# Two attentions in a hand-ordered kernel: row maxima 49 steps ahead of the scores instead of 64

## The reference

```
x = x + tanh(g_xattn[0]) * attention0(layernorm(x), context)     # 16 heads of 16, causal
x = x + tanh(g_ffn[0])   * moe0(layernorm(x))                    # 32 experts, top 8
x = x + tanh(g_xattn[1]) * attention1(layernorm(x), context)     # 16 heads of 16, row mask
x = x + tanh(g_ffn[1])   * moe1(layernorm(x))                    # 8 experts, top 2

scores  = q @ k.T / sqrt(16);  att = softmax(scores);  out = (att @ v) @ Wp + bp
```

## Time and profile before

| | us |
|---|---|
| median of three runs (2055.78 to 2060.46) | 2060.3 |
| the profiled execution, its own time | 2058.18 |
| its span, first to last instruction | 2056.1 |
| attention 0 with its set-up, about | 0 to 667 |
| experts 0, about | 667 to 902 |
| attention 1, about | 902 to 1574 |
| experts 1, about | 1574 to 2056 |
| mean granted TensorE clock | 0.946 |

### The profile page before, as it was taken

The page is one execution under the profiler, slowest core; times in us unless marked ns, Lnnn a source line. Parts: engine busy times, 40 slices in busy tenths (PEclk is TensorE's granted clock), DMA queues, the critical chain, the costliest instruction groups (busy, mean ns, idle before and its releaser), DMA issues. The chain is left out here.

```text
span 2056.1 us, 29834 instructions
## 1 busy us (share of the span) xinstructions
PE 1774.4 (86%) x10491; PEld 1061.7 (52%) x10491; DVE 1069.3 (52%) x2740; ACT 888.6 (43%) x1684; POOL 603.5 (29%) x580
## 2 busy tenths in 40 slices
PE   3799999889873999827899999999974999999995
PEld 1456555555542877713344444443332666666664
DVE  4556877787745644405877777778521122212221
ACT  3366665655541222223677777776750111111110
POOL 4222211210002678732211331231123244433322
PEclk9999999999985999968999999999986999999998
DMA  3535545334223788635323433332132133333314
GB/s 108 173 119 169 157 150 162 111 119 138 76 79 96 166 173 176 134 67 169 103 69 119 136 98 99 115 116 67 44 104 84 32 83 83 80 80 77 82 21 102
DMA packets 204243, 222.84 MB, mean 108 GB/s; under 512 B 33438, under 2 KB 195231, under 8 KB 203431
## 3 DMA queue, kind: packets, MB, share of 16 engines
q1 hardware_dynamic: 176458, 177.48, 28.3%
q0 software_dynamic: 27648, 43.60, 11.4%
HBM read 155.06 MB, written 86.93 MB: 118 GB/s over the span
## 5 line engine op out<-in xcount | busy, mean ns | idle before, releaser
L902 DVE TENSOR_REDUCE nmx<-mxb 128x1 f32<-128x512 f32 (+1 forms) x896 | 521.7, 609 | 238.9 <-PE mxb L673 145.8
L760 ACT ACTIVATE pt<-stb 128x512 f32<-128x512 f32 x832 | 475.2, 598 | 278.0 <-PE stb L693 154.4
L673 PE MATMUL mxb<-kst,qst 96*128 96x512 bf16 (+4 forms) x1024 | 334.6, 349 | 38.6 <-DVE nmx L902 28.2
L690 PE MATMUL stb<-qst,kst 99*128 99x512 bf16 (+4 forms) x1024 | 327.2, 344 | 8.6 <-DMA qst<-m3T 4.7
L706 PE MATMUL ob<-pt,va 128*32 128x512 f32 (+3 forms) x2048 | 220.1, 525 | 2.7 <-ACT pt L760 1.7
L690 PEld LDWEIGHTS stb<-qst,kst 102*128 102x128 bf16 (+1 forms) x1024 | 99.5, 99 | 213.5 <-ACT pt L760 136.7
L1192 POOL TENSOR_TENSOR qk<-qk,parts 128x512 f32<-128x512 f32 x64 | 73.0, 1161 | 431.0 <-ACT qk L795 226.2
L673 PEld LDWEIGHTS mxb<-kst,qst 99*128 99x128 bf16 (+1 forms) x1024 | 101.3, 99 | 152.1 <-DVE nmx L902 80.7
L1734 POOL DMA_INDIRECT x_after_l<-e_y,e_token x64 | 99.5, 1555 | 271.8 <-DVE e_y L1699 257.1
L1695 DVE TENSOR_TENSOR e_y<-e_y_bank,kst 128x512 f32<-128x512 f32 x32 | 22.1, 692 | 196.1 <-PE e_y_bank L1599 196.1
L1497 POOL DMA_INDIRECT x_after_l<-e_y,token x64 | 102.2, 1597 | 46.6 <-DMA x_after_l<-e_y,token 19.1
(11 more groups left out here) (252 smaller groups left out, 2959.2 us busy)
## 6 DMA issues: line engine op xcount, KB each, us to landing
qk_parts<-parts SPq DMA_DIRECT2D x16, 1536.0 KB, 6.3
qst<-qk_parts SPq DMA_DIRECT2D x384, 64.0 KB, 2.3
kst<-qk_parts SPq DMA_DIRECT2D x384, 64.0 KB, 2.3
rows<-rows SPq DMA_DIRECT2D x15, 1060.0 KB, 8.5
crow<-in_ctx SPq DMA_DIRECT2D x16, 512.0 KB, 3.9
x_after_l<-xres SPq DMA_DIRECT2D x16, 512.0 KB, 3.3
e_gu_nat<-in_L_ffn_gate_up_proj SPq DMA_DIRECT2D x64, 128.0 KB
qst<-in_L_ffn_w SPq DMA_DIRECT2D x8, 1024.0 KB, 7.2
```

Of the source, the lines that this page charges most:

```text
L673: last = pe.matmul(out, qst[par][0:rows_used, h, qt * P:(qt + 1) * P], kst[par][0:rows_used, h, 0:nk], start=True, stop=not causal)
L690: last = pe.matmul(bank[:, to:to + S - q_from(kt)], kst[par][0:ROWS, h, kt * P:(kt + 1) * P], qst[par][0:ROWS, h, q_from(kt):S], start=Tru ...
L760: act.activation(pt[:, slot(b, u), q0:S], stb[no % N_ST][:, q0:S], ACT.Exp, scale=SCALE).then_inc(s["st_free"], 1)
L902: last = dve.tensor_reduce(nmx[:, qt, h:h + 1], got[:, at:at + k_to(qt)], AX.X, ALU.max, negate=True)
```

## The change

The maxima run 15 steps later on every engine: `maxima(nxt, u - 15)` at step u, and the last 15 steps of an item are made in the item's own iteration, at steps 0 to 14. The steps of the shift move with them: first half - parts at 47 and 48, trip at 49, copy at 50; second half - parts at 15 and 16, trip at 17, copy at 18. Parts two and three now stand in one step, and the trip in the next. In SP's queue `load_ctx` goes ahead of `shift(cur, 1)`. Nothing is added or removed.

```diff
-    3: ("k", 2, 0, 0, 0), 4: ("k", 2, 0, 1, 0), 5: ("shift", 0, 1, 0, 1),
+    3: ("k", 2, 0, 0, 0), 4: ("k", 2, 0, 1, 0), 17: ("shift", 0, 1, 0, 1),
...
-    36: ("shift", 1, 0, 0, 0), 39: ("o", 0, 1, 0, 0), 40: ("y", -1, 0, 0, 1), 41: ("y", -1, 1, 0, 0),
+    49: ("shift", 1, 0, 0, 0), 39: ("o", 0, 1, 0, 0), 40: ("y", -1, 0, 0, 1), 41: ("y", -1, 1, 0, 0),
...
 STEPS = 64
+BEHIND = 15
...
                 if nxt is not None:
                     stack(nxt, 3)
+                if nn is not None and nn + 1 < B:
+                    load_ctx(nn + 1)
                 if cur is not None:
                     shift(cur, 1)
-                if nn is not None and nn + 1 < B:
-                    load_ctx(nn + 1)
...
                     if cur is not None:
                         scores(cur, u)
-                    if nxt is not None:
-                        maxima(nxt, u)
+                    if u < BEHIND and cur is not None:
+                        maxima(cur, u + STEPS - BEHIND)
+                    if u >= BEHIND and nxt is not None:
+                        maxima(nxt, u - BEHIND)
...
-                    if u == 6 and cur is not None:
+                    if u == 18 and cur is not None:
                         shift_out(cur, 1)
-                    if u == 37 and nxt is not None:
+                    if u == 50 and nxt is not None:
                         shift_out(nxt, 0)
...
-                    if nxt is not None and u in MAX_BANKS:
-                        maxima(nxt, u)
+                    if u < BEHIND and cur is not None and u + STEPS - BEHIND in MAX_BANKS:
+                        maxima(cur, u + STEPS - BEHIND)
+                    if u >= BEHIND and nxt is not None and u - BEHIND in MAX_BANKS:
+                        maxima(nxt, u - BEHIND)
...
-                    if u < 3 and cur is not None:
-                        shift_part(cur, 1, u)
+                    if u in (15, 16) and cur is not None:
+                        shift_part(cur, 1, u - 15)
+                    if u == 16 and cur is not None:
+                        shift_part(cur, 1, 2)
...
-                    if u in (32, 33, 34) and nxt is not None:
-                        shift_part(nxt, 0, u - 32)
+                    if u in (47, 48) and nxt is not None:
+                        shift_part(nxt, 0, u - 47)
+                    if u == 48 and nxt is not None:
+                        shift_part(nxt, 0, 2)
```

## The result

The changed kernel takes 2074.6 us, median of five runs (2070.9 to 2076.2), against 2056.0 us (2054.0 to 2060.5) for the kernel before in the same comparison: ratio 1.0081, 95% interval 1.0063 to 1.0099, so it is **slower by 0.8%**, which on 2056 us is 16.7 us. The forecast was no change: +1.3 us, 2062 us, with a range of 2050 to 2074. What came is the direction, the place and nearly the price of the second rival (2074 us), but, as the experiments show, not its cause.

A forecast was written before the change was run, and what follows sets the result against it. TensorE was taken to bound full iterations, VectorE's maxima attention 1's start and SP's queue attention 0's. Terms summed to +1.1 (attention 1) and +0.2 (attention 0), +1.3 us on the median 2060.3: 2062 us, range 2050 to 2074.

The forecast's parts named there:

- second rival: Slower: the trip at 17 stalls as well, VectorE 1 us behind in attention 0; +13, 2074 us; chance 0.18.
- attention 1: start: First score of attention 1 comes 6.4 us sooner, since iteration -1 loses 15 of 64 maxima; bounds 3.4 to 11.7.
- trip at 49: TensorE stalls 1.0 us for VectorE's split, net 0.75 in seven iterations of attention 1 (+5.3); 0.7 each in attention 0 (+4.9).
- trip at 17: Two output-projection trips cover the split; stall under 0.1 us, +0.7 over seven iterations of attention 1, 0 in attention 0.
- last iteration: 15 steps of maxima partly fill TensorE's waits in each attention's last iteration: +1.5 us in attention 1, +1.5 in attention 0.
- attention 0: start: SP's queue sends the second item's parts store at 82.5 us: gain 1.1 us at attention 0's start, bounds 0 and 2.0.
- "o" trip at 55: Attention 0, step 55: a maximum now ahead of two routing links delays this trip 0.4 us, six times: +2.4.
- `m3T` waits of "o" trips: The "o" trips behind the old places no longer wait for the shift's copy, nearly all in attention 0: -4.3 us.
- first steps' wait: Four iterations of attention 0: routing's last links begin a step earlier, removing 0.8 of TensorE's 1.20 us wait: -3.2 us.
- third rival: Clock stays low longer through attention 1's maxima and takes the start's gain: +4, and +5 together, 2066 us; chance 0.10.

The follow-up runs named there:

- e2: Changed kernel with the first half's shift trip at step 50 instead of 49 and its copy at 51 instead of 50; ratio to the kernel before 1.0021.
- e1: Changed kernel with GpSimd's subtraction for the keys' remainder waiting until the second half's split is through; 2060.9 us, ratio to the kernel before 1.0012.
- e10: Kernel before, with GpSimd's subtraction for the queries' remainder in attention 0 waiting until routing's last conversion is through; ratio to the kernel before 0.9967.
- e6: Changed kernel with maxima 13 steps behind, both splits two steps earlier, and GpSimd's keys' remainder waiting for the split; ratio to the kernel before 0.9993.
- e7: Changed kernel with the edits of both e1 and e2; ratio to the kernel before 0.9952.
- e3: The change in attention 1 alone, attention 0 keeping the order of the kernel before; ratio to the kernel before 1.0046.

## Why the prediction was wrong

Term by term, in us, from the two profiled executions (an iteration's waits are summed over TensorE's timeline):

| term | predicted | measured |
|---|---|---|
| attention 1: start | -6.4 | -7.2 |
| trip at 49, net | +5.3 | +6.7 (0.95 x 7, by e2) |
| trip at 17 | +0.7 | +4.2 |
| last iteration | +1.5 | +3.0 |
| attention 0: start | -1.1 | +0.4 |
| trip at 49 | +4.9 | +6.7 |
| "o" trip at 55 | +2.4 | 0 (0.26 longer four times, 0.53 shorter twice) |
| `m3T` waits of "o" trips | -4.3 | -4.3 |
| first steps' wait | -3.2 | -4.8 |
| trip at 17 | 0 | +9.0 |
| last iteration | +1.5 | +0.1, at a higher clock (below) |

Other waits of attention 0 that nobody priced (list trips, transposes of x, expert selection, output projection) fell by about 5 us.

- **The step that failed is the trip at step 17**: "two output-projection trips ... cover the split" was true for a split of 0.88 us, and the split measured was not the split that would run: in its new place it meets GpSimd. The prediction listed GpSimd's busy time but never asked what GpSimd runs at steps 14 to 16, and the introduction's "They meet at semaphores only" leaves no room for such a hold. The waits there are 13.2 us, against 0.7; with GpSimd's subtraction out of the way (e1) 3.5 us are left.
- **The second rival** named the place and the price rightly, and its test ("TensorE waits at the trip of step 17") was the one that came true. Its cause, VectorE in arrears, explains at most 1.28 and 1.16 us in the two first iterations (e1); the rest is the hold. That its sum came so near is luck: it has 0.5 us in fourteen iterations, where six have 0.8 to 3.0 us and the others 0.2 or less.
- **The first-steps wait** went, and more than counted, but for a reason that the forecast did not have. The links do "begin about a step earlier": in iteration 1 `lo_u` starts 2.1 us ahead of the next item's first exponential, where it started 0.8 us ahead. But what that brings is that the links are through, or nearly, when GpSimd's other subtraction begins, 0.8 us ahead of that exponential in both kernels. Moving that subtraction alone takes the waits away too (e10), and moving the links back beside it brings them back (e6).
- **The trip at 49** was read rightly in its gross size (1.0 forecast, 0.97 measured). The 0.25 us to be given back was not: the maximum of step 50 did come sooner, and the iteration was no shorter for it.
- **The last iterations.** Attention 1's 15 maxima cost 3.0 us, nearly their whole time (15 x 0.22 = 3.3). The prediction had 2 us of waits for them to fill, 11.0 less "about 9"; before, TensorE waits in these steps for 0.19, 0.20 and 0.30 us only. Attention 0's were not free: its last iteration had a clock of 0.92 before and 1.00 after, and in e1 and e7, at 0.96, it takes 1.4 us more than before, as forecast.
- **Attention 0's start.** The late store that the forecast set right was one execution's: in the other three traces with attention 0 in the old order it follows its load at once, and lands as late as after the change. Why a store that goes at once takes 1.7 us more was not tried.
- **The clock.** The third rival looked at the start of attention 1, and it did not decide there: the clock was at its lower level for 13.6 us in these maxima (before 17.1), and the start gained more than forecast. But in five iterations TensorE's work took 1 to 2 us longer, 8.2 us together. The sum of the two profiled executions is +17.0 us: waits of TensorE in the sixteen iterations +10.8 (53.3 to 64.1), those five stretches +8.2, work in the last iterations +4.8 and in the others +2.0, attention 1's start -7.2, attention 0's +0.4, and the untouched experts between the attentions -2.0. The 8.2 us are one execution's, and not all of them hang on the waits, as said above: in e3 the unchanged attention 0 lost 3.0 us in iteration 3 in this way behind its old waits. That a stall costs more than its length is not shown: e1 took away 9.7 us of waits at step 17 and gave back 14, but the intervals leave that difference open by some 4.5 us either way.

## What to carry to other kernels

A short chain of VectorE casts and subtracts in SBUF had its undisturbed time here only where no large GpSimd subtraction ran beside it: before moving such a chain, read GpSimd's timeline at the new place, and look in the groups of VectorE for operations whose longest time is far from their median (the subtract of the split after: shortest 191, median 192, longest 1087 ns). Where TensorE must wait for a chain in order, leave it two steps, as e2 did, and look at the granted clock behind a long stall. A gap in one trace can be that execution's alone, as the late store was: see it in a second one before pricing it. A wait put on the engine with idle time (GpSimd here) can buy more than reordering the busy ones: e10 alone gave 6.8 us.

## What the runs showed of the hardware that was not expected

- A cast of 128x32 elements and a subtract of the same size, 0.18 us alone, took up to 1.09 us beside GpSimd's 128x512 float subtraction and up to 0.65 beside its 128x256 one: held to the end of the one that runs. Between two such instructions one VectorE operation gets through. Reductions out of PSUM were not held (0.69 us beside it in e1).
- A 1.5 MB store issued 0.6 us behind a load landed after 8.8 to 9.1 us in eleven traces, and issued 1.6 us behind it after 7.1 in one: there, issuing it earlier gained nothing.
